# A twelve-block decoder on one core: from two steps of four batches to four chunks of two batches, merged slot by slot

## The reference

```
x = LN(x + silu(x @ W_G) * retention(x) @ W_O)     # "ret"   8 heads, decay mask
x = LN(x + cross attention(x, ctx, mask))          # "x0"    16 heads
x = LN(x + experts(x))                             # "moe0"  8 experts, hidden 512, top 2
x = LN(x + cosine attention(x) -> 3-layer MLP)     # "cos"
x = LN(x + single-head cross attention(x, ctx))    # "one"
x = LN(x + experts(x))                             # "moe1"  8 experts, hidden 256, top 1
x = LN(x + sparsemax attention(x))                 # "spm"   every row of 256 scores is sorted
x = LN(x + cross attention(x, ctx))                # "x2"
x = LN(x + base(x) + gated low-rank layer(x))      # "lora"
x = LN(x + LN'(32-head attention(x)))              # "big"
x = LN(x + cross attention(x, ctx, mask))          # "x3"
x = LN(x + quantized LN(x) @ ternary weights)      # "last"  one maximum over all tokens
```

## Time and profile before

| | |
|---|---|
| three runs | 1800.63, 1802.36, 1806.02 us; median 1802.36 us |
| the profiled execution | 1803.72 us, span of its instructions 1802.0 us |
| mean granted clock of PE | 0.828 of full speed |
| DVE busy | 1126.0 us, 62% of the span |
| ACT, POOL busy | 544.1 us (30%), 328.0 us (18%) |
| DMA | 16.89 MB, most of it in the first slice of 45 us |

### The profile page before, as it was taken

How to read it: one execution, slowest core, us unless ns; L and a number is a source line. 1 busy time by engine, 2 the same in 40 slices (tenths; PEclk the granted TensorE clock), 3 DMA queues, 4 the chain that set the end, 5 groups by cost and what they waited for, 6 DMA issues and landing times. The chain is left out here.

```text
span 1802.0 us, 25522 instructions
## 1 busy us (share of the span) xinstructions
PE 1253.0 (70%) x9712; PEld 877.5 (49%) x9712; DVE 1126.0 (62%) x2756; ACT 544.1 (30%) x985; POOL 328.0 (18%) x251
## 2 busy tenths in 40 slices
PE   6689987883435888776477999687353578878550
PEld 5457665552324565454354676565232355545330
DVE  5643324388964778875575333336988468878666
ACT  2132323331102555442203233143111135645120
POOL 6300001000001333331251000000000114333201
PEclk9789997986556999897788999798765679989775
DMA  7000000000000000000000000000000000000000
GB/s 303 1 1 1 1 1 1 1 1 0 1 0 1 1 1 2 1 2 1 14 1 1 1 1 1 1 1 1 1 1 0 1 1 2 2 1 2 0 1 24
DMA packets 5492, 16.89 MB, mean 9 GB/s; under 512 B 2920, under 2 KB 3448, under 8 KB 4600
## 3 DMA queue, kind: packets, MB, share of 16 engines
q1 hardware_dynamic: 5368, 15.21, 2.2%
HBM read 14.16 MB, written 1.05 MB: 8 GB/s over the span
## 5 line engine op out<-in xcount | busy, mean ns | idle before, releaser
L387 POOL TENSOR_TENSOR rstd<-var,minus_half 128x4 f32<-128x4 f32 x58 | 60.2, 1038 | 1000.4 <-DVE var L383 992.6
L2249 POOL TENSOR_TENSOR arena<-arena 128x1024 f32<-128x1024 f32 x64 | 150.8, 2356 | 269.1 <-ACT arena L2166 269.1
L1162 PEld LDWEIGHTS banks<-WS,arena 128*128 128x128 f32 x1536 | 183.1, 194 | 26.3 <-issue 25.3
L1199 PE MATMUL banks<-XT,WS 128*128 128x512 f32 x384 | 189.5, 630 | 6.6 <-DVE R L1316 6.6
L1162 PE MATMUL banks<-WS,arena 128*128 128x128 f32 x1536 | 184.9, 278 | 0.0
L428 PE MATMUL banks<-ident,X 128*128 128x128 f32 x176 | 44.9, 408 | 199.3 <-DVE X L393 167.2
L2183 DVE TENSOR_REDUCE arena<-banks 128x4 f32<-128x1024 f32 x128 | 150.7, 1219 | 25.4 <-PE banks L2063 23.7
L1254 ACT ACTIVATE arena<-banks,BC 128x512 f32<-128x512 f32 x160 | 108.6, 688 | 176.1 <-PE banks L1199 175.8
L2166 ACT ACTIVATE arena<-banks 128x1024 f32<-128x1024 f32 x128 | 124.3, 1021 | 109.0 <-PE banks L2086 109.0
L1316 DVE SCALAR_TENSOR_TENSOR R<-banks,arena,R 128x128 f32<-128x128 f32 x256 | 72.1, 344 | 134.2 <-PE banks L1162 132.1
L463 ACT COPY arena<-banks 128x512 f32<-128x512 f32 x108 | 63.0, 585 | 280.7 <-PE banks L1452 89.1
(11 more groups left out here) (308 smaller groups left out, 2388.2 us busy)
## 6 DMA issues: line engine op xcount, KB each, us to landing
WS<-in_weights SPq DMA_DIRECT2D x3, 2048.0 KB, 17.7
WS<-in_weights SPq DMA_DIRECT2D x1, 2368.0 KB, 30.3
RW<-in_rows SPq DMA_DIRECT2D x1, 1032.0 KB
XALL<-in_x SPq DMA_DIRECT2D x1, 1024.0 KB, 7.8
out_dram<-arena SPq DMA_DIRECT2D x4, 256.0 KB, 2.4
WS<-in_weights SPq DMA_DIRECT2D x1, 900.0 KB, 19.2
WS<-in_weights SPq DMA_DIRECT2D x1, 645.0 KB, 24.2
WS<-in_weights SPq DMA_DIRECT2D x1, 580.0 KB, 8.9
```

The costliest lines, as they stand in the source:

```text
L1162: ins = PE.matmul(v[:, tile(t)], self.HT[:, i % 2, j, tile(t)], self.W2[:, e, j], start=j == 0, stop=j == self.J - 1)
L1199: PE.matmul(v, self.W1[:, e, j], XT[:, chunk(c)], start=True, stop=True)\
L2249: G.tensor_tensor(big.ES[:, n % 2], big.E[:, n % 2, :, 0], big.E[:, n % 2, :, 1], ALU.add).then_inc(pool.flag("big.sums"), 1)
```

## The change

The batches are now four chunks of two batches (`CB` = 2), the loop is gone, and the program is one straight line for each engine. Every block is a set of four generator functions, one for each engine, that `yield` at the same slots. A list `ORDER` says which chunk and block has the next slot; every engine's program is made by stepping the generators in the order of this list. `weave` merges two threads of slots in proportion to the time that a table `SLOTS` gives each slot.

```diff
+CB = 2
+CHUNKS = B // CB
+SLOTS = {
+    "ret": [1.5, 3.5] + even(10, 2) + [3, 2.5, 2],
+    "moe0": [2, 3] + even(8, 6) + [2],
+    "spm": [2.5, 3, 2] + even(9, 5.2) + [5.5, 2, 3, 2],
...
+def weave(*threads):
+    slots = []
+    for thread in threads:
+        total, at = sum(sum(SLOTS[stage]) for _, stage in thread), 0
+        for i, stage in thread:
+            for us in SLOTS[stage]:
+                slots.append(((at + us / 2) / total, len(slots), i, stage))
+                at += us
+    return [(i, stage) for _, _, i, stage in sorted(slots)]
...
+ORDER = weave(stages(0, "ret", "x0"))
+ORDER += weave(stages(0, "moe0", "cos", "one", "moe1"), stages(1, "ret", "x0"))
+for _i in range(2):
+    ORDER += weave(stages(_i, "spm", "x2", "lora"), stages(_i + 1, "moe0", "cos", "one", "moe1"))
+    ORDER += weave(stages(_i, "big"))
+    ORDER += weave(stages(_i, "x3"), stages(_i + 2, "ret", "x0"))
+ORDER += weave(stages(2, "spm", "x2", "lora"), stages(3, "moe0", "cos", "one", "moe1"))
+ORDER += weave(stages(2, "big"))
+ORDER += weave(stages(2, "x3"), stages(3, "spm", "x2", "lora"))
+ORDER += weave(stages(3, "big"))
+ORDER += weave(stages(3, "x3"))
...
-        with nc.Fori(0, STEPS) as step:
...
-            clear_counts()
...
+        def run(which, engine_of):
+            live = {}
+            for i, stage in ORDER:
+                if (i, stage) not in live:
+                    live[i, stage] = STAGES[stage][which](engine_of(i), i)
+                next(live[i, stage])
```

Inside the blocks little changes. Retention multiplies the keys on POOL once for each batch and uses 32-row groups of PE for the scores, where before it masked them for each of the head pairs and used all 128 rows:

```diff
-                    PE.matmul(v[:, hh, 0:256], key[:, 0:128], ret.QT[:, b * S:b * S + S], start=True, stop=True)
...
+                        ins = PE.matmul(v[:, hh, at:at + S - P * key_block],
+                                        ret.KM[rows_of, b, heads[hh] % 2, tile(key_block)],
+                                        ret.QT[rows_of, b * S + P * key_block:b * S + S], start=True, stop=True)
```

More of the change, by code:

```diff
@@ new lines, in pe @@
+                v = psum.take(pe, f"{L}.v{i}")
+                for b in range(CB):
+                    ins = PE.matmul(v[:, tile(b)], CD[:, CB * i + b, :], self.w("Wv"), start=True, stop=True)
+                ins.then_inc(psum.filled(f"{L}.v{i}"), 1)
+                x_t_ready(pe, self.before, i)
+                v = psum.take(pe, f"{L}.q{i}")
+                PE.matmul(v, self.w("Wq"), XT[:, slot(i)], start=True, stop=True).then_inc(psum.filled(f"{L}.q{i}"), 1)
+                yield
+                self.maxima_pe(pe, i, 0)
@@ new lines, in cos_pool, with one_pe @@
+            add_bias_pool(pool, "cos", "moe0", "L1_attn_b3", i)
+            yield
+            yield from idle(6)
+            yield from end_slots_pool(pool, "cos", i)
+        def one_pe(pe, i):
+            pe.wait_ge(*psum.copied(f"one.k{i}"))
+            x_t_ready(pe, "cos", i)
+            v = psum.take(pe, f"one.s{i}")
+            for t in range(4):
+                ins = PE.matmul(v[:, t * SK:t * SK + SK], XT[:, slot(i), tile(t)], one.KT[:, t // 2, :],
+                                start=True, stop=True)
+            ins.then_inc(psum.filled(f"one.s{i}"), 1)
+            yield
+            pe.wait_ge(*psum.copied(f"one.s{i}"))
+            v = psum.take(pe, f"one.pT{i}")
@@ L1930, in lora_pe @@
+        def lora_pe(pe, i):
             w0 = W_AT["L2_ffn_gate_w"][0]
[L1931 to L1938 removed]
@@ L2012, in lora_pool @@
-        def lora_pool(pool):
-            add_bias_pool(pool, "lora", "x2", "L2_ffn_base_b")
-            end_pool(pool, "lora")
-        GROUPS = NB * 8
+            x_t_ready(pe, "x2", i)
+            for half in range(2):
+                v = psum.take(pe, f"lora.lz{i}{half}")
+                for t in range(2):
+                    ins = PE.matmul(v[:, t * 138:t * 138 + 138], XT[:, slot(i), tile(2 * half + t)],
+                                    WS[:, w0:w0 + 138], start=True, stop=True)
+                ins.then_inc(psum.filled(f"lora.lz{i}{half}"), 1)
@@ new lines, in lora_pe @@
+            yield
+            yield
+            pe.wait_ge(sig("lora.z"), i + 1)
+            turn_pe(pe, "lora.z", lora.LZ[:, :, 10:138], i)
+            yield
+            pe.wait_ge(*psum.copied(f"lora.zT{i}"))
+            v = psum.take(pe, f"lora.out{i}")
+            for t in range(4):
+                PE.matmul(v[:, tile(t)], XT[:, slot(i), tile(t)], W("L2_ffn_base_w"), start=True, stop=False)
+                ins = PE.matmul(v[:, tile(t)], lora.ZT[:, tile(t)], W("L2_ffn_lora_B"), start=False, stop=True)
```

2635 lines of the change are left out of this document (1153 added, 1482 removed).

## The result

| | before | after |
|---|---|---|
| runs beside each other, median | 1802.36 us (1800.63 to 1806.02) | 1791.67 us (1790.50 to 1796.10) |
| ratio | | 0.9948, 95% interval 0.9935 to 0.9961 |
| span of the profiled execution | 1802.0 us | 1788.6 us |
| mean granted clock | 0.828 | 0.821 |

The change makes the kernel faster by 0.5%, 11 us. I had forecast 109 us.

The account below looks back on a forecast made before the run. No engine bounds the whole: PE and DVE take turns, and chains bound x2 and lora. Phases sum 90+178+540+480+168+155+44+38 = 1693 us, also the predicted time; range 1570 to 1815.

Parts of the forecast that it names:

- the surcharge of the merges: Large merges: other thread's work in front adds +2 in moe0, +6 in cosine attention, +5 beside moe1; together 180 us.
- How I sum: Every phase: the larger of longer thread alone and fuller engine, plus what the other thread puts in front.
- The merges of x3 with ret and x0: x3 beside a later chunk's ret and x0: 78 us thread, +6 for x3 in front, 84, twice 168.
- The threads' lengths: Threads alone for one chunk: moe0 to moe1 167.6 us; sparsemax, x2, lora 137; retention plus x0 78.
- The 32-head attention: Four times alone: 5.75 us a group, 120 us each with filling and uncovered tail, 480 in all.
- Rival 1: Merges: engines and not chains bound them; 152 us each, about 1555 us in all; chance 0.20.
- Rival 2: Merges: in-order coupling makes them slower; 1871 us; chance 0.20.
- the first half: moe0 beside the sort: PE's second layer waits for the sort slot, rounds 10.6 us not 7.3, +26 a merge.
- the second half: Cosine attention: it and the other thread add up and do not overlap, +33 us each, 99 in all.
- Rival 3: Sort steps: DVE and POOL block each other, about 6 us a merge, +18, 1711 us; chance 0.05.
- The first matmul: Kernel start: PE starts at 12 us again, since POOL's setup is the same.
- The clock: Large merges: PE near full clock, above 0.8 in sort stretches, perhaps 6 us less a merge, 1675 in all.

Follow-up runs that it names:

- serial run: The kernel after with every weave of two threads replaced by the two threads one behind the other, slots unchanged: 2142.22 us.
- calib: The kernel after with only the table SLOTS changed, to the slot lengths seen in the serial run: 1769.85 us, ratio 0.9808 to before.
- swap: The kernel after with moe0's last slot put in front of the eighth sort slot in each large merge: 1781.86 us, ratio 0.9889 to before.
- pace_p2: The kernel of calib with the large merges' slots placed by absolute time instead of by share: 1823.38 us, ratio 1.0101 to before.
- order_one: The kernel after with weaves replaced by a searched slot order, the same on every engine, 32-head tail free to move: 1668.05 us, ratio 0.9247 to before.
- final_start: The kernel of order_four after further order exchanges, with SP's DMA issues moved from the setup block to the second block: 1646.91 us, ratio 0.9137 to before.
- order_four: As order_one, but each of the four engines has its own searched slot order in the merges: 1653.21 us, ratio 0.9163 to before.

## Why the prediction was wrong, step by step

- **The step that failed** is the surcharge of the merges, in "How I sum": the larger of the longer thread and the fuller engine, plus what the other thread puts in front. I put +12.4 us on the expert thread's 167.6 (rounded from +2 in moe0, +6 in the cosine attention, +5 beside moe1). Measured between the same marks of the serial run it is 11 in moe0, 8 in the cosine attention, 4 in the single-head attention and 17 beside moe1, 40 in all, and 33 in the first merge instead of 11. With the three large merges that is 93 of the 96 us; the other phases are off by +38 and -36 us and nearly cancel. The merges of x3 with ret and x0 show the same fault: ret and x0 alone are 80.4 us, merged 92, so x3 costs 11 to 12 us and not the +6 that I gave it. I had looked for full engines and for one dear slot in front of a chain. Of the 40 us of a large merge 8.6 go with the sort, 3.4 with one exchanged slot, 17 with another common order and 26 with an order for each engine; these overlap, and the 14 that no order took away stay open.
- **It is the order and not the work.** calib (-25 us), swap (-11), pace_p2 (+28) and order_one (-126, by ratio against after) have the same instructions. With the searched order the whole comes out near my sum, 1666.8 us of span in order_one against 1693, but not phase by phase: the large merges are 187.5 us and not 180, the first 183 and not 178, while the 32-head attention with x3, ret and x0 is 191 and not 204, where its tail was free to move, and x3 of chunk 3 with the last block 65 and not 82. That near agreement of the total is luck, and that another order comes near the forecast does not make it right for this one: I counted what the work allows, and the program's order was in front of me.
- **The threads' lengths**, built from rows of before, were within 2% for the experts; sparsemax's thread was 15 us too long, 9 of them in x2. Its 38 us were not those of one chunk alone: between 529.04 and 567.08 us PE also did the end of the other chunk's x2 (output product at 552.93, transposition at 558.71), 23.2 us of work where x2 alone has 17.7. x3 with sparsemax, forecast at 155, took 136 (the thread alone 127), and x3 of chunk 3 with the last block 65 instead of 82: these two hid 36 us of the error.
- **The 32-head attention**: pace 5.75 us as in the earlier trace rows, and the hole behind its output product is there, 10.2 us of PE's wait (I had said some 15). Alone the block is 126.9 us from its first projection to the transposition (622.67 to 749.54) and not 120, in after 121 to 127. The missing 7 us are in filling and draining: in the serial run the last maxima are at 716.92 us and the transposition at 749.54, 33 us later, of which product and normalizations are the 18 that I had counted. The four together were sized too low by 17 us.
- **Rival 1** (engines bound the merges) fell: 157 us of PE in 204. **Rival 2**: the first half did not happen, PE's rounds beside the sort stayed at 7.0 us, as the rows below show, with DVE busy 55.3 of the 63 us from 725 to 788; the second half did in part. I gave 33 us to the cosine attention alone if the threads add up; measured, 28 us are lost over the whole merge beyond my terms. Its second half was the right mechanism in kind, and I gave it 0.20 because I thought of it only as all or nothing.

```profile
743.96 3.60 PE L1102 MATMUL banks<-XT,WS 128*128 128x512 f32 x8
...
750.97 3.60 PE L1102 MATMUL banks<-XT,WS 128*128 128x512 f32 x8
```

- **Rival 3**: lines 1642 and 1643 are at 698 and 699 ns, against 692 and 685 of the two lines in the serial run, 3 us in all (144 of each). One place shows what there is of it, DVE's and POOL's rows of after:

```profile
805.24 1.75 DVE L1643 TENSOR_TENSOR arena<-arena 128x512 f32<-128x512 f32 x1
```

```profile
804.85 1.60 POOL L500 TENSOR_TENSOR XB<-XALL,RW 128x512 f32<-128x512 f32 x1
```

  A sort step that meets POOL's sum takes 1.75 us instead of 0.69, and ends after it. The Trainium skill, "SBUF — State Buffer", "Who interferes with whom", says that such a pair blocks each other; the trace agrees here, and the price is small because it seldom happens: of the 288 sort steps only three took over 1 us (1.75, 1.75 and 1.63, one in each large merge, in the cosine attention), and from 725 to 788 us, beside moe0, POOL did nothing. I had put 6 us a merge under this risk; it is some 1 us. The mean of 1706 ns in the earlier trace rows hides the same thing: of its four, two took 0.69 us and two 2.72, the first of these from 735.27 us on, 0.4 us behind the start of a POOL product of 2.60 us.
- **The first matmul**: forecast at 12, seen at 18.2, because I took POOL's setup for what ends last and did not count SP's issues, which the change moves into the setup block.
- **The clock**: 0.84 in the large merges of after, 0.88 in order_one's. PE was granted 0.99 beside the sort in moe0 (725 to 788 us), above the 0.8 that I had named, and the merges are longer than forecast all the same. Over a whole merge the 0.84 is not the full clock that I had hoped for, and 6 us a merge would be too few to see in one that is 24 us too long. PE's busy time is 1265.9 us in after and 1244.6 in order_one for the same instructions; how much of the 126 us this higher clock gives, and how much the order alone, no run tells apart. The Trainium skill, "TensorE: Matmul & The Clock Gate", Part 1, has the low clock as the state of idleness; the traces agree in that the shorter merge, with the same work and less idle time, has the higher clock.

## What to carry to other kernels

Two dependent chains that are woven slot by slot on in-order engines cost more here than the longer of them, even where no engine is full: take each thread alone from one serial run, and do not expect all of the shorter one to be hidden. Here the four kinds of merge hid between half and two thirds of it in the woven order, and the searched orders four fifths and more in the large merges (99 and 108 of 122 us). Then look at what stands in front of each wait (here a 5.2 us slot between a variance and its normalization made a merge 3.4 us longer), and try the order itself before the work: here it was worth more than ten times what the restructuring had brought. The border of a block can hold the engines too: here PE started at 18.2 us while SP issued DMAs in the setup block until 17.7, and at 12.1 us once they stood in the next block.

## What was not expected of the hardware

- A DVE operation of 0.69 us was held to 1.75 by a POOL operation that had begun 0.4 us before it.
- The issue of a DMA took SP 0.35 to 0.46 us at the start, but 0.69 to 2.03 us for the mask transfers of single elements, and 0.9 us for each of the six weight transfers behind them (5.33 us). In final_start, issued in the second block, the mask transfers took 0.63 to 0.70 us each.
- Given its own order, each engine gains something over one common order, but less than the order itself: order_four is 0.0084 below order_one (15 us).
